# Attention into experts on one core: two late pairs instead of three, the last pair's values by halves, a GpSimd piece and a gather moved, and the last products regrouped

## What is computed

```python
x = x + xattn(layernorm(x), ctx)          # 16 x 128 x 256
#   normed = rmsnorm(hn);  v = [normed, ctx]
#   attn = softmax(mask(q(normed) @ k(v).T));  h_tilde = attn @ v
#   out = (1 - alpha) * hn + alpha * h_tilde,  alpha = sigmoid(gate(hn))
y = layernorm(x)                           # rows of 256
for e in range(8):                         # tok = top_idx[:, e], 512 rows
    h = gelu(y[tok] @ W1[e] + b1[e])       # 512 x 1024
    out[tok] += (h @ W2[e] + b2[e]) * combine[tok, e]
x = x + out
```

## Time and profile before

| what | value |
|---|---|
| median of three runs | 274.85 us |
| the profiled execution: its time, and its span | 275.01 us, 273.2 us |
| TensorE, VectorE, ScalarE, GpSimd busy | 97%, 80%, 69%, 57% of the span |
| mean granted TensorE clock | 0.996 |
| first expert product (line 1370) starts | 83.51 us |
| last product ends (268.77 + 0.28) | 269.05 us |
| VectorE: x2 addition of pair 6, gate logits of pair 7 | 71.86 + 0.69 us, 72.47 + 0.87 us |
| VectorE's last low part of pair 7 ends (81.43 + 0.42) | 81.85 us |
| SP issues pair 6's x2 store, the last lists (line 349) | 72.58 us, 82.08 us |

### The profile page before, as it was taken

One profiled execution on the slowest core, in us unless ns is written; L12 is line 12 of the kernel. 1 busy time (PEld: TensorE's weight loads), 2 busy tenths in 40 slices (PEclk: granted clock), 3 DMA queues, 4 the chain that ended last, 5 costly groups with the idle time before them and its releaser, 6 DMA issues.

```text
span 273.2 us, 5127 instructions
## 1 busy us (share of the span) xinstructions
PE 263.7 (97%) x1477; PEld 225.8 (83%) x1477; DVE 218.4 (80%) x553; ACT 188.2 (69%) x349; POOL 156.9 (57%) x152
## 2 busy tenths in 40 slices
PE   7899999999989999999999999999999999999993
PEld 3688899999876888888888888888888888888983
DVE  1899999899985779968878896796887889689453
ACT  2687899887666975786676587668657758773540
POOL 4349765565768717656456466655645656514525
PEclk9999999999999999999999999999999999999998
DMA  5986257588446945454464544645446561210211
GB/s 154 341 232 199 94 154 200 148 231 270 133 149 150 388 154 157 129 169 155 134 208 154 156 142 135 168 118 207 160 138 180 160 181 56 59 35 34 65 49 69
DMA packets 30560, 42.44 MB, mean 155 GB/s; under 512 B 5521, under 2 KB 24283, under 8 KB 30416
## 3 DMA queue, kind: packets, MB, share of 16 engines
q1 hardware_dynamic: 25120, 29.74, 35.0%
q0 software_dynamic: 4608, 12.24, 15.4%
q10 hardware_dynamic: 816, 0.26, 0.4%
HBM read 33.54 MB, written 9.24 MB: 157 GB/s over the span
## 4 chain that ended last, share of the span: by engine, by line
PE 81%; DVE 6%; issue 4%; DMA 4%; POOL 1%; ACT 1%; SPq 0%; DVEq 0%; POOLq 0%
PE bank L1423 19%; PE bank L1202 12%; PE bank L1203 12%; PE bank L1204 12%; PE bank L1424 10%; PE bank L1250 4%; PE bank L1294 3%; DMA x_all<-in_x_dram 2%; PE bank L1351 2%; DMA x_all<-token_rows,idx_all 2%; PE bank L1370 1%; PE bank L1371 1%; PE bank L1374 1%; PE bank L1318 1%; POOL out_dram L557 1%
## 5 line engine op out<-in xcount | busy, mean ns | idle before, releaser
L752 ACT ACTIVATE keysT<-bank,biasT 128x512 f32<-128x512 f32 x63 | 43.6, 692 | 55.6 <-PE bank L1204 39.3
L557 POOL DMA_INDIRECT out_dram<-h,sidx x32 | 36.7, 1146 | 40.2 <-DVE h L1094 34.8
L547 POOL DMA_INDIRECT x_all<-out_dram,idx_all x32 | 36.6, 1143 | 23.6 <-DMA out_dram<-h,sidx 16.0
L1202 PE MATMUL bank<-x_hi,w_parts 128*128 128x512 f32 (+1 forms) x114 | 45.1, 396 | 0.0
L1203 PE MATMUL bank<-x_lo,w_parts 128*128 128x512 f32 (+1 forms) x114 | 44.4, 389 | 0.0
L1204 PE MATMUL bank<-x_hi,w_parts 128*128 128x512 f32 (+1 forms) x114 | 44.1, 387 | 0.0
L1119 DVE TENSOR_TENSOR g_lo<-keysT,g_hi 128x512 fp32r<-128x512 f32 x32 | 22.1, 692 | 27.0 <-ACT g_hi L753 26.3
L543 POOL DMA_INDIRECT x_all<-token_rows,idx_all x28 | 30.7, 1095 | 18.9 <-DVE factor L1143 12.4
L1423 PE MATMUL bank<-w_parts,g_hi 128*128 128x512 f32 x112 | 40.5, 396 | 0.0
L1124 DVE TENSOR_TENSOR w_parts<-w_raw,w_parts 128x512 fp32r<-128x512 f32 x56 | 38.4, 686 | 0.0
L758 ACT CAST w_parts<-w_raw 128x512 fp32r<-128x512 f32 x56 | 34.9, 623 | 0.0
(11 more groups left out here) (187 smaller groups left out, 681.5 us busy)
## 6 DMA issues: line engine op xcount, KB each, us to landing
w_raw<-in_L_ffn_W_dram SPq DMA_DIRECT2D x32, 512.0 KB
idx_rows<-in_L_ffn_top_idx_dram SPq DMA_DIRECT2D x8, 256.0 KB, 4.1
out_dram<-x SPq DMA_DIRECT2D x8, 256.0 KB, 2.9
hn_cnat<-in_ctx_dram SPq DMA_DIRECT2D x7, 256.0 KB, 2.8
token_rows<-xn SPq DMA_DIRECT2D x7, 256.0 KB, 2.2
hn_cnat<-in_L_ffn_b_dram SPq DMA_DIRECT2D x1, 1024.0 KB
x_all<-in_x_dram SPq DMA_DIRECT2D x3, 256.0 KB, 6.8
x_all<-in_x_dram SPq DMA_DIRECT2D x1, 768.0 KB, 9.4
```

Of the source, the lines that this page charges most:

```text
L547: g.indirect_dma_start(accg[:, t, :], None, flat, list_of(e, t)).then_inc(acc_in[t], 16)
L557: g.indirect_dma_start(flat, idx(sidx[:, t:t + 1].bitcast(U32), 0), newrow[:, t, :], None, bounds_check=N - 1, oob_is_err=False).then_inc( ...
L752: a.activation(g32[:, f % NG, :], ps_up[f % 2][:, :], ACT.Gelu_apprx_tanh, bias=bias)
L1202: t_.matmul(dst, lhs_hi, rhs_hi, start=first, stop=False)
```

## The change

- `EARLY_PAIRS` goes from 5 to 6. Pair 5's rows are stored to HBM by SP and gathered with the others; its eight late products, its cast on ScalarE, its low part on VectorE and its two `onehot` matrices are gone. Two products of a zero matrix (`junk`) open the banks instead.
- For pair 5's rows (made while pair 6 is in attention): VectorE runs `stats2` and `aggr2` ahead of the gate logits, and `shift` ahead of the next h rows; ScalarE makes the next query's copy and then the normalised rows ahead of tanh.
- GpSimd's low part of weight piece 5 (`expert0_lo`) moves from between `normed` and `rstd` of pair 6 to behind pair 7's `x_plus_h`, ahead of the gathers.
- Gathers: two, then `rstd` of pair 6, the third, the power of pair 7's first half, the fourth, the power of the second half.
- Pair 7: the transposes of its probabilities go by halves, the first between the two halves of its gate product; ScalarE copies each half, and the values product of a half waits for that half alone.
- The late products are regrouped so that both banks get their last product next to each other.
- SP: the loads of chunks 2 and 3 of expert 1's weights move behind the load of b2.

```diff
-    EARLY_PAIRS = NPAIR - 3
+    EARLY_PAIRS = NPAIR - 2
...
# SP
                 if r == LAST - 1:
                     for t in range(NT):
                         sp.wait_ge(first_rows_in[t], 16)
-                    for late in (LAST - 2, LAST - 1):
-                        sp.wait_ge(xn_rdy, 2 * late + 2)
-                        sp.dma_start(rows_v[:, 2 * late:2 * late + 2, 0:H], xn2[:, late % 2, :, :])\
-                            .then_inc(xn_out[late % 2], 16)
+                    sp.wait_ge(xn_rdy, 2 * r + 2)
+                    sp.dma_start(rows_v[:, 2 * r:2 * r + 2, 0:H], xn2[:, r % 2, :, :]).then_inc(xn_out[r % 2], 16)
...
-                if r % 2 == 1:
+                if r in (1, 3):
                     sp.wait_ge(wlo0_rdy, r + 1)
                     load_chunk(1, r // 2)
             sp.wait_ge(pv_mm, NPAIR)
             row_broadcast(b2_bc, b2.rearrange("e h -> (e h)")).then_inc(b2_in, 16)
+            for c in range(2, NCH):
+                sp.wait_ge(wlo0_rdy, 2 * c + 2)
+                load_chunk(1, c)
...
# GpSimd, attention
                 if is_last(p):
-                    gather_first_rows(range(NT - 1))
+                    expert0_lo(LAST - 2)
+                    gather_first_rows(range(2))
...
-                    if not is_last(p):
+                    if not is_last(p) and not is_last_but_one(p):
                         expert0_lo(p - 1)
                     rstd(p - 1, 1 - s)
                 if is_last(p):
-                    gather_first_rows(range(NT - 1, NT))
+                    gather_first_rows(range(2, NT - 1))
...
-            for b in range(2):
-                last_rstd(b)
+            last_rstd(0)
+            gather_first_rows(range(NT - 1, NT))
+            last_rstd(1)
...
# ScalarE, attention
-                if is_last(p):
-                    act.wait_ge(xn_rdy, 2 * p - 2)
-                    act.wait_ge(q_mm, NPAIR)
-                    a.copy(late_hi[0], xn2[:, s, :, :]).then_inc(late_hi_rdy, 1)
...
-                act.wait_ge(pT_mm, p + 1)
-                a.copy(probsT, ps_pT).then_inc(pT_ev, 1)
+                if is_last(p):
+                    for b in range(2):
+                        act.wait_ge(last_pT_mm, b + 1)
+                        a.copy(probsT[:, b, :, :], ps_pT_last[b]).then_inc(last_pT_ev, 1)
+                else:
+                    act.wait_ge(pT_mm, p + 1)
+                    a.copy(probsT, ps_pT).then_inc(pT_ev, 1)
...
+                if is_last_but_one(p):
+                    query(p + 1)
+                    normalised_x2(p - 1, 1 - s, use - 1)
                 act.wait_ge(gate_rdy, 2 * p + 2)
...
# VectorE, attention
-                    if not is_last(p):
+                    if not isinstance(p, int):
...
                         one_hot(p - 1)
                     mix(p - 1)
                     residual(p - 1, 1 - s, last_use)
+                    if is_last_but_one(p):
+                        stats2(p - 1, 1 - s)
+                        aggr2(p - 1, 1 - s)
...
-                    aggr2(p - 1, 1 - s)
+                    if is_last_but_one(p):
+                        shift(p - 1, 1 - s)
+                    else:
+                        aggr2(p - 1, 1 - s)
                     if not is_last(p):
                         h_rows(p + 1, 1 - s)
...
-                if is_last(p):
-                    dve.wait_ge(late_hi_rdy, 1)
-                    dve.wait_ge(xn_rdy, 2 * LAST - 2)
-                    v.tensor_tensor(late_lo[0], xn2[:, s, :, :], late_hi[0].bitcast(F32), ALU.subtract)\
-                        .then_inc(late_lo_rdy, 1)
...
# TensorE
+            def last_probs_transposed(b):
+
+                if b == 0:
+                    pe.wait_ge(pT_ev, NPAIR - 1)
+                pe.wait_ge(exp_rdy, 2 * LAST + b + 1)
+                for j in range(2):
+                    last = t_.transpose(ps_pT_last[b][:, j, :], probs[:, b, j * S:(j + 1) * S], ident[:, :])
+                last.then_inc(last_pT_mm, 1)
...
+                    if is_last(p) and b == 0:
+                        last_probs_transposed(0)
```

More of the change, by code:

```diff
@@ L157, in build_xattn_moe @@
         list0_f = idx_rows[:, (IDX_PARTS - 1) * C:IDX_PARTS * C].bitcast(F32)
-        late_hi = [M_hi[:, :, :], gateT_hi[:, :, :], hnT_hi[:, 0, :, :]]
-        late_lo = [M_lo[:, :, :], gateT_lo[:, :, :], hnT_lo[:, 0, :, :]]
+        late_hi = [gateT_hi[:, :, :], hnT_hi[:, 0, :, :]]
+        late_lo = [gateT_lo[:, :, :], hnT_lo[:, 0, :, :]]
         xn_last = qT
@@ L301, in each_pair, with is_last_but_one @@
             body(LAST, 1, 3)
+        def is_last_but_one(pair):
+            return isinstance(pair, int) and pair == LAST - 1
         def has_second_next(pair):
@@ L397, in _ @@
                     load_ctx(r + 3)
[L398 removed]
+                if r == EARLY_PAIRS - 3:
                     sp.wait_ge(xh_rdy, r + 1)
@@ L694, in attention @@
                     hn_rows(p + 3, 1 - s)
-                if not is_first(p):
+                if not is_first(p) and not is_last_but_one(p):
                     normalised_x2(p - 1, 1 - s, use if s == 1 else use - 1)
@@ L964, in attention @@
                     x_stats(10, NB, 4)
-                else:
+                elif not is_last_but_one(p):
                     stats2(p - 1, 1 - s)
@@ L984, in attention @@
                     dve.wait_ge(x_steps, steps[0])
-                elif not is_last(p):
+                elif not is_last(p) and not is_last_but_one(p):
                     shift(p - 1, 1 - s)
@@ L1271, in attention @@
                         .then_inc(setup_mm, 1)
-                pe.wait_ge(exp_rdy, 2 * p + 2)
-                for b in range(2):
-                    for j in range(2):
-                        last = t_.transpose(ps_pT[:, b, j, :], probs[:, b, j * S:(j + 1) * S], ident[:, :])
-                last.then_inc(pT_mm, 1)
+                if is_last(p):
+                    last_probs_transposed(1)
+                else:
+                    pe.wait_ge(exp_rdy, 2 * p + 2)
+                    for b in range(2):
+                        for j in range(2):
+                            last = t_.transpose(ps_pT[:, b, j, :], probs[:, b, j * S:(j + 1) * S], ident[:, :])
+                    last.then_inc(pT_mm, 1)
                 if not is_last(p):
@@ L1280, in attention @@
                     hn_transposes(2, 0)
-                if is_last(p):
-                    pe.wait_ge(log_rdy, 2 * NPAIR - 1)
-                    pe.wait_ge(late_hi_rdy, 1)
-                    for b in range(2):
-                        late_rows(0, b, late_hi, first=b == 0)
-                pe.wait_ge(pT_ev, p + 1)
+                if not is_last(p):
+                    pe.wait_ge(pT_ev, p + 1)
                 pe.wait_ge(n_rdy, p + 1)
@@ L1290, in attention @@
                 for b in range(2):
+                    if is_last(p):
+                        pe.wait_ge(last_pT_ev, b + 1)
                     for j in range(2):
@@ L1312, in early_rows, with late_rows @@
                                   start=False, stop=False)
-            def late_rows(n, b, part, first=False):
+            def late_rows(n, b, part):
                 pe.wait_ge(onehot_rdy, 2 * n + b + 1)
@@ L1318, in late_rows @@
                     t_.matmul(ps_xT[k][:, :], part[n][:, b, k * P:(k + 1) * P], onehot[:, 2 * n + b, :],
-                              start=first, stop=False)
+                              start=False, stop=False)
             each_pair(pe, attention)
-            early_rows(range(1))
+            pe.wait_ge(log_rdy, 2 * NPAIR - 1)
+            for k in range(KH):
+                t_.matmul(ps_xT[k][:, :], junk[:, 0:P], junk[:, :], start=True, stop=False)
+            early_rows(range(2))
+            pe.wait_ge(late_hi_rdy, 1)
+            for b in range(2):
+                late_rows(0, b, late_hi)
+            early_rows(range(2, 3))
+            pe.wait_ge(late_hi_rdy, 2)
+            late_rows(1, 0, late_hi)
             pe.wait_ge(late_lo_rdy, 1)
```

43 lines of the change are left out of this document (19 added, 24 removed).

## The result

| | before | changed |
|---|---|---|
| median of 16 runs each, us | 274.76 (274.27 to 275.51) | 275.99 (275.42 to 276.83) |
| profiled execution, us / span | 275.01 / 273.2 | 276.53 / 274.7 |

The ratio is 1.0047, 95% interval 1.0038 to 1.0057: 1.2 us slower, just inside the half per cent that the forecast called no change, 1.2 over the forecast of 274.75 and just above the upper end of its range, 275.9.

What follows compares the result with a forecast made beforehand. TensorE, busy 97%, bounds the kernel; only moving the first expert product counts. 0.94 us fewer products are offset by a later gather and awaited cast; regrouping gives 0.1: 275.01 to 274.9, less 0.16 to the median, 274.75 us, range 273.6 to 275.9.

Steps and rivals of the forecast that it cites:

- X: Moment TensorE has bank 0 complete, before the first expert product: 82.74 us before the change, forecast 82.75.
- the hand-over: From attention to expert 0, through the first gather: forecast to start at 71.75 and land 5.22 us later, at 76.95.
- the cast: ScalarE's cast of pair 6's high part (gateT_hi), behind gelu's table: ready at 78.05 plus table delay, TensorE wants it at 77.8.
- The low part beside the masks: GpSimd's moved low part holds VectorE's mix until 71.6; gelu's table, and so X, comes 0.13 us later.
- The second rival: Low part holds VectorE: mix ends 0.9 us later, X = 83.35, time 275.35; chance 0.27 together with the late store.
- The regrouping: TensorE's last late products: bank 1 complete 0.23 us after bank 0 instead of 0.7, worth 0.1 us, at least nothing.
- Moved at no cost: Moved gate logits, tanh, weight chunks and last lists cost nothing; lists issued at 82.8 land at 86.5, cover left 0.4 us.
- The chunks: Weight chunks 2 and 3 behind b2 on SP: ScalarE first reads chunk 2 over 5 us after it would land.
- The clock: Rival: TensorE idles 1.9 us before the first gather lands and its clock falls, costing 2.7 us, 277.4; chance 0.03.
- The landing rival: First gather takes 2.9 to 4 us, pair 7's halves set X at about 82.0, time 274.0; chance 0.22.

Runs made afterwards that it cites:

- Experiment 5: Changed kernel with the last lists loaded two rounds earlier, b2 left where the change put it; 275.31 us, ratio 1.0013 to the kernel before.
- experiment 10: Lists early and six zero products, with piece 5's low part back ahead of the power for pair 5's rows; 275.33 us, ratio 1.0024 to the kernel before.
- experiment 11: Changed kernel with lists early and six zero products, its last six late products back in the old order; 274.28 us, ratio 0.9990 to the kernel before.
- Experiments 1: Changed kernel with b2 and the two weight chunks waiting for expert 0's last low part; 275.40 us, ratio 1.0024 to the kernel before.
- experiment 3: Kernel before with b2 loaded right behind the last lists and the fourth weight chunk after it; 275.08 us, ratio 1.0015 to the kernel before.
- 6 again: The changed kernel with lists early and six zero products, timed again on another chip; 274.60 us, ratio 1.0000 to the kernel before.
- 7: Changed kernel with six more zero products ahead of the first gathered tile, lists not moved; 275.62 us, ratio 1.0042 to the kernel before.
- 2: Changed kernel with the third weight chunk right behind the lists, then the fourth chunk and b2 last; 275.89 us, ratio 1.0031 to the kernel before.
- 6: Changed kernel with the last lists two rounds earlier and six more zero products ahead of the first gathered tile; 274.37 us, ratio 0.9987 to the kernel before.
- experiment 8: Changed kernel with lists early, third weight chunk back behind pair 5's store, fourth chunk and b2 last; 276.15 us, ratio 1.0041 to the kernel before.
- experiment 4: Kernel before with expert 1's third weight chunk loaded at 86 us with the fourth and b2; 275.63 us, ratio 1.0031 to the kernel before.
- 9: Changed kernel with lists early, third chunk behind pair 5's store, fourth chunk and b2 last, plus six zero products; 274.95 us, ratio 1.0001 to the kernel before.

## Why the prediction was wrong, and where it held

On before's clock, 0.31 is added to the changed kernel's times.

- **X, and the hand-over (right, partly by cancelling errors).** Forecast 82.75. ScalarE's first x_hi cast starts at 82.52 against 82.77 before, so X is 82.80 against 82.74. The store of pair 5's rows was issued at 69.03, for 69.1, and landed in 2.18, for 2.2. The gather started at 72.13, for 71.75: GpSimd needed 0.92 after the store's landing before it started. In the sum nothing stood for that. It landed in 4.52 (76.34 - 71.82), for 5.22, which took 0.7 back. gateT_hi was ready at 77.96, for 78.18; from there to X it took 4.84, for 4.55. So what decided is what the forecast named, the cast. Experiment 5 bears it out: its gather landed in 3.9, TensorE then waited 0.53 for gateT_hi, and those products started 49.22 after A, against 49.25 in the changed kernel. That X came within 0.05 is luck: the gather's start, its landing, the cast (which held 0.13 for a delay that did not come) and the time behind it were off by 0.2 to 0.7 each, in both directions. The Trainium skill's fit for a DMA from GpSimd's queue ("DMA: Bandwidth & Descriptors", anatomy of one DMA), an estimate of 2.3 us, is met by neither gather here: 4.52, and 2.86 for the fourth.
- **The low part beside the masks (wrong in time, harmless).** The mix was to be held until 71.6. `x_plus_h` started 0.91 after the shift, not 1.2, and the shift was itself 0.15 early, so the low part ended 0.04 before the mix started (GpSimd's, then VectorE's timeline):

```profile
68.25 1.28 POOL L512 TENSOR_TENSOR x_plus_h<-x_all,h 128x512 f32<-128x512 f32 x1 [0.94 <-DVE h L845]
69.49 1.27 POOL L505 TENSOR_TENSOR w_parts<-w_raw,w_parts 128x512 fp32r<-128x512 f32 x1
71.82 1.46 POOL L499 DMA_INDIRECT x_all<-token_rows,idx_all  x1 [1.05 <-DMA token_rows<-xn]
```

```profile
67.34 0.16 DVE L931 SCALAR_TENSOR_TENSOR shift<-mv,rstd 128x2 f32<-128x2 f32 x1
...
70.80 0.69 DVE L900 SCALAR_TENSOR_TENSOR diff<-setup_or_probs,diff 128x512 f32<-128x512 f32 x1
```

The mix took 0.69, and tanh came at 73.34, for 73.67 (73.54 and the 0.13). The second rival rested on the same collision and fell with it. By experiment 10 the place is worth 0.66.

- **"The regrouping. … Worth 0.1; at least nothing" (wrong in sign).** It shortens F to T by the 0.1 that was forecast (11.57 against 11.66 in experiment 11), and lengthens A to F by 0.47, which is two products (0.234 each) of the second bank that now stand ahead of bank 0's end. The sum for X did contain those two products, which is why the total was right; the part was credited with its gain and never charged for them. By the traces it costs 0.38 alone; without it, and with the lists early and the zero products, the other edits gain 0.46 (240.01 - 239.55).
- **"Moved at no cost": "landed at 86.5 with 3.7 … Cover left 0.4" (the step that failed).** The issue was right (82.50 + 0.31 = 82.81, for 82.8), and the cover nearly (0.6: 86.80 less 82.50 and 3.7). The duration was not, 5.6 for 3.7: the earlier trace rows has it with nothing right behind it on SP, and the change itself puts 1 MB 0.5 us behind it. With chunk 3 moved behind b2, b2 no longer waits for the low parts, and the forecast never asked what b2 does when it leaves over 3 us earlier. The 1.9 more use up the cover and leave ScalarE 1.35 short, TensorE 1.2. The forecast priced the two moves on SP each by itself and did not lay them on top of one another. Experiments 1 (3.5 without b2 behind it, and no wait) and 3 (5.1 with it, in the kernel before) show the cause. Moving the lists alone gives it back (1.0 us in the time, experiments 6 again and 7).
- **The chunks: "over 5 us after it would land" (true, and not the question).** ScalarE never waited for w_raw. But the forecast asked only for whom the moved bytes are late, not whom they delay. In the changed kernel that is the last lists. In experiments 1 and 2 it is expert 1's first gathers, wanted at 95.2, by 0.4 and 0.8 us. The changed kernel shows no such wait, and neither do experiments 5 and 6, which issue b2 and the chunks in its order and have TensorE on time. How much beside the gathers is too much stays open: the kernel before has chunk 3 and b2 there (86.0 and 86.4) and no wait.
- **The clock (0.03, 2.7 us).** Against it stood that it never fell in a gap so far. It did fall in 2 of 16 runs of the changed kernel, 3 of 12 of experiments 1 and 2 each, 6 of 12 of experiment 5 and 8 of 11 of experiment 8, and in none of the 103 of the kernel before beside the experiments; the price, from one trace of experiment 5, is 1.45. It does not set the changed kernel's median.
- **The landing rival** did not come true: the gather did not land in 2.9 to 4, and in experiment 4 the absence of pair 5's chunk did not speed it. In experiment 5 it did land so early, and gateT_hi then held TensorE at the same time after A; pair 7's halves did not set X there.

## What to carry to other kernels

When a change moves a load and also what is issued behind it, take the load's landing from a row with that much traffic behind it, or bound it there: bytes that are late for nobody can make others late. Moving the delayed load ahead of them worked here; moving them behind it made the next loads late. When the last products fill two banks, keep one bank's products to run under the cast of the other. Before comparing two traces by absolute time, cut both at a mark ahead of the change: 0.31 us of chance looked like a gain here.

## What the runs showed of the hardware

- A load on SP's queue was delayed by a larger one issued 0.5 us behind it: 256 KB took 3.5 to 3.8 us with nothing behind it for 3 us, 4.1 with 512 KB behind it, 5.1 with 1 MB of b2, and 5.3 and 5.6 with b2 and 512 KB more. The Trainium skill ("DMA: Bandwidth & Descriptors", queues, rings and completion order) says that each DMA engine consumes the descriptors of a ring in order, but that a later one may finish its write before an earlier one; it has no figure for what that costs the earlier transfer. The runs have one; by what mechanism it comes they don't tell.
- GpSimd started expert 0's first gather 0.91 to 0.93 us after the landing of the store it waited for, in the seven traces whose chain shows both (changed, experiments 1, 2, 7, 8, 9, 10). Behind an arithmetic operation of its own a gather starts after 0.18 to 0.22, behind another gather after 0.30.
- The length of TensorE's gap does not by itself tell whether the granted clock falls. With 1.02 us (before), 0.98 (experiment 3) and 1.28 (experiment 4) it fell in no run, with 1.07 and 0.53 close together (experiment 5) in half of them, with 1.70 and 0.20 (changed) in two of 16, with 1.78 and 1.84 (experiments 1 and 2) in three of twelve, with 2.23 (experiment 8) in eight of eleven. But for experiment 5 the gaps are those of an execution at full clock. What decides stays open. With six products of zeros, 1.46 us of work, it fell in none of the runs that the ratios compare, in all five kernels that had them.
